# The attention's normalised rows: split as rows and turned by transposing transfers, instead of turned by TensorE and split from PSUM

## What is computed

```python
x = x + wkv_block(layernorm(x))     # k, r = h@Wk.T, h@Wr.T; scan over time per channel; sigmoid(r)*y @ Wo.T
x = x + ffn_block(layernorm(x))

def ffn_block(x):
    h = rmsnorm(x, gamma1)
    q = h @ Wq + bq                          # 16 heads of 32
    k, v = split((h @ Wdown + bdown) @ Wup + bup)   # latent of 64, then 16 heads
    att = softmax(q k^T / sqrt(32))          # between the 16 heads of one token
    x = x + att v @ Wo + bo
    h2 = rmsnorm(x, gamma2)
    return x + sum_e gate_e * (h2 @ We[e])   # 8 experts, all of them, dense
```

## Time and profile before

| | us |
|---|---|
| median of three runs | 2759.6 |
| the profiled execution, its time | 2758.6 |
| its span, first to last instruction | 2756.5 |
| TensorE busy with matmuls | 2586.4 (94%), 18896 matmuls |
| VectorE busy | 2133.6 (77%) |
| ScalarE busy | 1531.3 (56%) |
| GpSimd busy | 948.9 (34%) |
| mean granted TensorE clock | 0.975 of full speed |

### The profile page before, as it was taken

One profiled execution on the slowest core, in us unless ns is written; L12 is line 12 of the kernel. 1 busy time (PEld: TensorE's weight loads), 2 busy tenths in 40 slices (PEclk: granted clock), 3 DMA queues, 4 the chain that ended last, 5 costly groups with the idle time before them and its releaser, 6 DMA issues.

```text
span 2756.5 us, 48625 instructions
## 1 busy us (share of the span) xinstructions
PE 2586.4 (94%) x18896; PEld 1580.4 (57%) x18896; DVE 2133.6 (77%) x3647; ACT 1531.3 (56%) x2799; POOL 948.9 (34%) x970
## 2 busy tenths in 40 slices
PE   2458999999999999999999999999999999999999
PEld 2345566666556666655666665566666556655554
DVE  6677887788888778788877878887787888767743
ACT  5875555555555555555555555556555555654540
POOL 0453433333333333243333324333332433332420
PEclk7768999999999999999999999999999999999999
DMA  7202222211222221122222112222112222201220
GB/s 229 39 12 39 47 47 47 32 27 37 47 47 47 47 30 28 38 47 47 47 47 25 33 38 47 47 47 47 23 33 40 47 47 47 46 12 37 39 32 16
DMA packets 845322, 119.29 MB, mean 43 GB/s; under 512 B 813587, under 2 KB 813715, under 8 KB 845075
## 3 DMA queue, kind: packets, MB, share of 16 engines
q1 hardware_dynamic: 845092, 116.18, 22.9%
HBM read 48.49 MB, written 16.78 MB: 24 GB/s over the span
## 4 chain that ended last, share of the span: by engine, by line
PE 88%; DVE 4%; ACT 4%; POOL 2%; SPq 1%; issue 1%; DMA 0%; ACTq 0%; DVEq 0%; POOLq 0%
PE bank L1333 78%; PE bank L1355 3%; PE bank L1500 2%; PE bank L1471 2%; PE bank L1511 2%; DVE h2t L1104 1%; PE bank L1487 1%; POOL w_e L693 1%; ACT h2t L939 1%; PE bank L1512 1%; ACT ot L789 1%; DVE mcol L1234 0%; ACT t L888 0%; POOL pr L734 0%; DVE acc L1311 0%
## 5 line engine op out<-in xcount | busy, mean ns | idle before, releaser
L1333 PE MATMUL bank<-w_e,h2t 128*128 128x512 f16 x6144 | 1383.4, 380 | 2.8 <-DVE acc L1311 2.0
L1333 PEld LDWEIGHTS bank<-w_e,h2t 128*128 128x128 f16 x6144 | 592.1, 98 | 665.9 <-issue 4.4
L1311 DVE SCALAR_TENSOR_TENSOR acc<-bank,gates,acc 128x512 f32<-128x512 f32 x512 | 371.9, 736 | 120.4 <-PE bank L1333 117.4
L906 ACT ACTIVATE pr<-bank,plog,col 128x512 f32<-128x512 f32 x256 | 198.7, 776 | 407.9 <-PE bank L1500 405.5
L734 POOL TENSOR_TENSOR pr<-pr 128x512 f16<-128x512 f32 x256 | 295.7, 1160 | 182.3 <-ACT pr L908 180.9
L721 POOL TENSOR_TENSOR qo<-t,qo 128x256 f16<-128x256 f32 x128 | 106.5, 832 | 493.4 <-ACT qo L891 490.3
L1142 DVE TENSOR_TENSOR_SCAN wkv<-e,wkv 128x256 f32<-128x256 f32 x256 | 210.8, 864 | 74.6 <-ACT e L834 73.4
L1166 DVE RECIPROCAL zz<-zz 128x256 f32<-128x256 f32 x128 | 218.9, 1732 | 29.4 <-POOL zz L703 29.3
L1333 PE MATMUL bank<-w_o,xo 128*128 128x512 f16 x768 | 176.2, 387 | 46.9 <-DVE xo L1104 46.9
L908 ACT ACTIVATE pr<-bank,plog,col 128x512 f16<-128x512 f32 x256 | 197.8, 773 | 0.0
L1333 PE MATMUL bank<-xo,w_k 128*128 128x256 f16 x1536 | 172.9, 273 | 2.4 <-DVE xo L1104 2.4
(11 more groups left out here) (196 smaller groups left out, 3957.6 us busy)
## 6 DMA issues: line engine op xcount, KB each, us to landing
qs<-qo SPq DMA_DIRECT2D x384, 64.0 KB, 2.4
ks<-k SPq DMA_DIRECT2D x384, 64.0 KB, 2.4
xk<-in_attn_x SPq DMA_DIRECT2D x32, 512.0 KB, 4.0
x<-in_attn_x SPq DMA_DIRECT2D x32, 512.0 KB, 3.7
result<-acc SPq DMA_DIRECT2D x32, 512.0 KB, 2.8
w_e<-in_ffn_We SPq DMA_DIRECT2D x7, 1024.0 KB, 12.9
qs<-in_attn_Wk SPq DMA_DIRECT2D x1, 1024.0 KB, 7.9
ks<-in_attn_Wr SPq DMA_DIRECT2D x1, 1024.0 KB, 10.0
```

The source lines that it names most:

```text
L906: nc.scalar.activation(pr[:, k % 2, :], att_bank[ATT_BANK["S", k]][:, :], ACT.Exp, bias=plog[:, 0:1], scale=colof["soft"])\
L1311: V.scalar_tensor_tensor(out=acc[:, s, :], in0=moe_bank[u % 2][:, :], scalar=gates[:, s, e:e + 1], in1=acc[:, s, :], op0=ALU.mult, op1=ALU ...
L1333: ins = nc.tensor.matmul(dst, left(a), right(b), start=(n == 0), stop=(n == last))
```

## The change

ScalarE's `att_turn` no longer reads PSUM. It copies the rows `h_rows`, scaled, as fp16 into `hr16[:, 0, s]`; VectorE writes the rest into `hr16[:, 1, s]`. `hr16` is not a new buffer, it is `k16` under another shape; so ScalarE first waits until the stacking transfers of the tile before have read `k16`. SP then issues four transfers with `transpose=True` in a tile, each of 128 rows by 512 fp16 (128 KB), one for each `s` and half, into `ht16`. TensorE's `att_turn` is gone from its lists, `att_latent` waits for the four transfers, and the two uses T0 and T1 leave the ring of banks. SP's lists have a new step `att_turn` ahead of `att_up`. The orders of ScalarE, VectorE and GpSimd are as before.

```diff
-ATT_USES = ([("T", 0), ("T", 1), ("D", 0), ("Q", 0), ...
+ATT_USES = ([("D", 0), ("Q", 0), ...
 PE_ORDER
-    ... ("mix_k", 0, 1), ("att_turn", 0, 2), ("mix_v", 0, 1), ("att_latent", 0, 2), ...
+    ... ("mix_k", 0, 1), ("mix_v", 0, 1), ("att_latent", 0, 2), ...
 SP_ORDER = [
-    ("mix_k", 0, 2), ("att_m", 0, 3), ("att_up", 0, 2), ("pre_load", 0, 0), ("moe_store", 0, 4),
+    ("mix_k", 0, 2), ("att_m", 0, 3), ("att_turn", 0, 2), ("att_up", 0, 2), ("pre_load", 0, 0), ("moe_store", 0, 4),
+        hr16 = k16[:, :, :, :].rearrange("p l b t -> p l (b t)").rearrange("p l (s c) -> p l s c", s=SUB)
+        turn1_in = Steps(sem("turn1_in"), 16, h=4)
 # SP
+            def att_turn(t, _):
+                if t.back(1):
+                    sp.wait_ge(*att_dve.done(t.back(1), "vt"))
+                for s in range(SUB):
+                    for l, (steps, step) in enumerate(((att_act, "h_hi"), (att_dve, "h_lo"))):
+                        sp.wait_ge(*steps.done(t, step, s))
+                        sp.dma_start(ht16[:, l, :, s * P:(s + 1) * P], hr16[:, l, s, :], transpose=True).then_inc(turn1_in.sem, 16)
 # ScalarE
             def att_turn(t, _):
-                for b in range(2):
-                    act.wait_ge(*att_pe.done(t, f"T{b}"))
-                    nc.scalar.activation(ht16[:, 0, 2 * b:2 * b + 2, :], att_bank[ATT_BANK["T", b]][:, :], ACT.Copy, scale=XS)\
-                        .then_inc(att_act.sem, 1)
+                if t.back(1):
+                    act.wait_ge(*stack_in.done(t.back(1), "qk"))
+                for s in range(SUB):
+                    act.wait_ge(*att_act.done(t, "h", s))
+                    nc.scalar.activation(hr16[:, 0, s, :], h_rows[:, s, :], ACT.Copy, scale=XS).then_inc(att_act.sem, 1)
 # VectorE
             def att_turn(t, _):
-                for b in range(2):
-                    dve.wait_ge(*att_act.done(t, "h_hi", b))
-                    lo(ht16[:, 1, 2 * b:2 * b + 2, :], att_bank[ATT_BANK["T", b]][:, :], XS, ht16[:, 0, 2 * b:2 * b + 2, :])\
-                        .then_inc(att_dve.sem, 1)
+                for s in range(SUB):
+                    dve.wait_ge(*att_act.done(t, "h_hi", s))
+                    lo(hr16[:, 1, s, :], h_rows[:, s, :], XS, hr16[:, 0, s, :]).then_inc(att_dve.sem, 1)
 # TensorE
-            def att_turn(t, _):
-                pe.wait_ge(*att_act.done(t, "h"))
-                turn(h_rows, [att_bank[ATT_BANK["T", b]] for b in range(2)], att_pe, att_pe.sem, lambda b: att_free(t, "T", b))
             def att_latent(t, _):
-                pe.wait_ge(*att_dve.done(t, "h_lo"))
+                pe.wait_ge(*turn1_in.done(t, "h"))
```

More of the change, by code:

```diff
@@ L114, in blocks @@
     return range(CB) if name in ("d", "g") else range(2 * k, 2 * k + 2)
-ATT_USES = ([("T", 0), ("T", 1), ("D", 0), ("Q", 0), ("Q", 1), ("K", 0), ("K", 1), ("V", 0), ("V", 1),
+ATT_USES = ([("D", 0), ("Q", 0), ("Q", 1), ("K", 0), ("K", 1), ("V", 0), ("V", 1),
              ] + [("M", k) for k in range(8)] + [("S", 0)]
@@ L142 @@
     ("set_o1", 1, -1), ("mix_k", 0, 0), ("mix_v", 0, 0), ("mix_project", 0, 0), ("mix_turn", 0, 1), ("mix_k", 0, 1),
-    ("mix_v", 0, 1), ("att_turn", 0, 0), ("att_latent", 0, 0), ("att_q", 0, 0), ("att_up", 0, 0), ("att_max", 0, 0),
+    ("mix_v", 0, 1), ("att_latent", 0, 0), ("att_q", 0, 0), ("att_up", 0, 0), ("att_max", 0, 0),
     ("att_max", 1, 0), ("att_max", 2, 0), ("att_max", 3, 0), ("att_m", 0, 0), ("att_scores", 0, 0),
@@ L147 @@
     ("att_scores", 6, 0), ("att_probs", 5, 0), ("att_scores", 7, 0), ("mix_project", 0, 1), ("mix_turn", 0, 2),
-    ("att_probs", 6, 0), ("att_probs", 7, 0), ("mix_k", 0, 2), ("att_turn", 0, 1), ("mix_v", 0, 2),
+    ("att_probs", 6, 0), ("att_probs", 7, 0), ("mix_k", 0, 2), ("mix_v", 0, 2),
     ("att_latent", 0, 1), ("att_q", 0, 1), ("fin_project", 0, 0), ("att_up", 0, 1), ("fin_turn2", 0, 0),
@@ L158 @@
     ("att_probs", 4, 3), ("att_scores", 6, 3), ("att_probs", 5, 3), ("att_scores", 7, 3), ("mix_project", 0, 2),
-    ("att_probs", 6, 3), ("att_probs", 7, 3), ("mix_turn", 0, 1), ("moe", 9, 4), ("mix_k", 0, 1), ("att_turn", 0, 2),
-    ("mix_v", 0, 1), ("att_latent", 0, 2), ("att_q", 0, 2), ("moe", 10, 4), ("att_up", 0, 2), ("moe", 11, 4),
+    ("att_probs", 6, 3), ("att_probs", 7, 3), ("mix_turn", 0, 1), ("moe", 9, 4), ("mix_k", 0, 1), ("mix_v", 0, 1), ("att_latent", 0, 2), ("att_q", 0, 2), ("moe", 10, 4), ("att_up", 0, 2), ("moe", 11, 4),
     ("moe", 12, 4), ("fin_project", 0, 3), ("moe", 13, 4), ("moe", 14, 4), ("moe", 15, 4), ("fin_turn2", 0, 3),
@@ L171 @@
     ("moe", 9, 5), ("mix_turn", 0, 2), ("att_probs", 6, 4), ("att_probs", 7, 4), ("moe", 10, 5), ("mix_k", 0, 2),
-    ("mix_v", 0, 2), ("att_turn", 0, 3), ("fin_project", 0, 4), ("att_latent", 0, 3), ("att_q", 0, 3),
+    ("mix_v", 0, 2), ("fin_project", 0, 4), ("att_latent", 0, 3), ("att_q", 0, 3),
     ("att_up", 0, 3), ("moe", 11, 5), ("moe", 12, 5), ("moe", 13, 5), ("fin_turn2", 0, 4), ("moe", 14, 5),
@@ L179 @@
     ("att_probs", 5, 3), ("att_scores", 7, 3), ("moe", 8, 4), ("mix_turn", 0, 1), ("moe", 9, 4), ("att_probs", 6, 3),
-    ("att_probs", 7, 3), ("mix_k", 0, 1), ("mix_v", 0, 1), ("att_turn", 0, 2), ("moe", 10, 4), ("moe", 11, 4),
+    ("att_probs", 7, 3), ("mix_k", 0, 1), ("mix_v", 0, 1), ("moe", 10, 4), ("moe", 11, 4),
     ("att_latent", 0, 2), ("att_q", 0, 2), ("att_up", 0, 2), ("fin_project", 0, 3), ("moe", 12, 4), ("moe", 13, 4),
@@ L187 @@
     ("att_scores", 6, 2), ("att_probs", 5, 2), ("att_scores", 7, 2), ("mix_project", 0, 1), ("att_probs", 6, 2),
-    ("att_probs", 7, 2), ("moe", 7, 3), ("moe", 8, 3), ("moe", 9, 3), ("att_turn", 0, 1), ("moe", 10, 3),
+    ("att_probs", 7, 2), ("moe", 7, 3), ("moe", 8, 3), ("moe", 9, 3), ("moe", 10, 3),
     ("att_latent", 0, 1), ("att_q", 0, 1), ("att_up", 0, 1), ("fin_project", 0, 2), ("moe", 11, 3), ("moe", 12, 3),
@@ L379 @@
     ("pre_load", 0, 1), ("set_experts", 6, -1), ("set_experts", 7, -1), ("set_masks", 0, -1), ("mix_k", 0, 1),
-    ("att_up", 0, 0), ("att_m", 0, 0), ("pre_load", 0, 2), ("att_up", 0, 1), ("pre_load", 0, 3),
+    ("att_turn", 0, 0), ("att_up", 0, 0), ("att_m", 0, 0), ("pre_load", 0, 2), ("att_turn", 0, 1), ("att_up", 0, 1), ("pre_load", 0, 3),
 ]
 SP_ORDER = [
-    ("mix_k", 0, 2), ("att_m", 0, 3), ("att_up", 0, 2), ("pre_load", 0, 0), ("moe_store", 0, 4),
+    ("mix_k", 0, 2), ("att_m", 0, 3), ("att_turn", 0, 2), ("att_up", 0, 2), ("pre_load", 0, 0), ("moe_store", 0, 4),
 ]
 SP_TAIL = [
-    ("mix_k", 0, 3), ("att_m", 0, 4), ("att_up", 0, 3), ("pre_load", 0, 1), ("moe_store", 0, 5), ("mix_k", 0, 2),
-    ("att_m", 0, 3), ("att_up", 0, 2), ("moe_store", 0, 4), ("mix_k", 0, 1), ("att_m", 0, 2), ("att_up", 0, 1),
+    ("mix_k", 0, 3), ("att_m", 0, 4), ("att_turn", 0, 3), ("att_up", 0, 3), ("pre_load", 0, 1), ("moe_store", 0, 5), ("mix_k", 0, 2),
+    ("att_m", 0, 3), ("att_turn", 0, 2), ("att_up", 0, 2), ("moe_store", 0, 4), ("mix_k", 0, 1), ("att_m", 0, 2), ("att_turn", 0, 1), ("att_up", 0, 1),
     ("moe_store", 0, 3), ("att_m", 0, 1), ("moe_store", 0, 2), ("moe_store", 0, 1),
@@ L556, in att_reader @@
         def att_reader(use, k):
-            return {"T": (att_dve, "h_lo", k), "D": (att_act, "c", 0), "Q": (att_act, "q", 4 * k + 2),
+            return {"D": (att_act, "c", 0), "Q": (att_act, "q", 4 * k + 2),
                     "K": (att_act, "k", 4 * k + 2), "V": (att_act, "v", 2 * k + 1),
@@ L672, in _ @@
                      {"set_ident": set_ident, "set_load": set_load, "set_experts": set_experts, "set_masks": set_masks,
-                      "pre_load": pre_load, "mix_k": mix_k, "att_up": att_up, "att_m": att_m, "moe_store": moe_store})
+                      "pre_load": pre_load, "mix_k": mix_k, "att_turn": att_turn, "att_up": att_up, "att_m": att_m, "moe_store": moe_store})
             sp.wait_ge(*stored.done(Tile(NT - 1, 1, 0), "out"))
@@ L1549, in _ @@
                      {f"set_{name}": lambda _, k, name=name: set_turn(name, k) for name in TURNED} | {"mix_turn": mix_turn, "mix_k": mix_k, "mix_v": mix_v, "mix_project": mix_project,
-                          "att_turn": att_turn, "att_latent": att_latent, "att_q": att_q, "att_up": att_up, "att_max": att_max, "att_m": att_m, "att_scores": att_scores, "att_probs": att_probs,
+                          "att_latent": att_latent, "att_q": att_q, "att_up": att_up, "att_max": att_max, "att_m": att_m, "att_scores": att_scores, "att_probs": att_probs,
                           "fin_project": fin_project, "fin_turn2": fin_turn2,
```

## The result

The changed kernel takes 2904.9 us, the median of four runs (2900.1 to 2906.6), against 2759.6 us before: a ratio of 1.0525 with an interval of 1.0507 to 1.0543. It is slower, on the side and inside the range that were forecast; the forecast of 2860 us gave about two thirds of the loss: +100 against +145 us.

A forecast was written before the change was run, and what follows sets the result against it. TensorE was taken as the bound: stall less transposes over 28 tiles 68 us, tail 4.5, clock 34, together +106 us on the median of 2759.6, rounded down to 2860 us; range 2742 to 3040 us.

The forecast's parts named there:

- The removed transposes are worth 0.87 us a tile: TensorE's chain: the eight transposes of a tile cost 0.87 us; alone, their removal would give 27 us over 31 tiles.
- The stall, S = 3.3 us: Before att_latent: TensorE waits 3.3 us a tile for the last of the four transposing transfers.
- i: On SP: the spacing of two transposing transfers, taken as 1.1 us from the pace of small packets.
- L: The landing time of one transposing transfer, taken as 2.9 us.
- The clock, 1.2 us a tile: TensorE after the stall: half of a mean price of 2.5 us for a clock fall, 34 us over 28 tiles.
- Tiles 1 to 28 alike: Same sequence in each of these tiles: 28 x (3.3 - 0.87) = 68 us lost, plus the clock term.
- Tile 0 is covered: Head: tile 0 gains and loses nothing, since ScalarE comes to the latent's copy only at 116.89.
- The tail, 4.5 us: Last three tiles: somewhat more cover, stall 2.4 us and 1.5 us lost each, 4.5 us together.
- A, ordinary price: Before att_latent: transfers move like plain 64 KB ones, stall 1.6 us, +20 us, 2780 us; chance 0.22.
- B: Before att_latent: last transfer lands before TensorE arrives, or nearly; faster, 2733 us with full cover; chance 0.12.
- C: Before att_latent: transfers in 32 B pieces, stall 7.8 us and a clock fall each period, 3047 us; chance 0.16.
- D: Before att_latent: transfers turned block after block, none overlapped, stall 26 us, 3530 us; chance 0.05.

The follow-up runs named there:

- the best kernel: Changed kernel with halves made earlier, two transfers of 256 KB in place of four, and the same moves in head and tail lists: 2745.2 us, ratio 0.9950.
- the kernel with idle matmuls: Changed kernel with 24 idle matmuls in TensorE's list between mix_v and the wait for the four transfers: 2863.4 us, ratio 1.0376.
- the one with earlier halves: Changed kernel with ScalarE's and VectorE's att_turn earlier in the repeated lists and SP issuing the two hi transfers first: 2773.9 us, ratio 1.0053.
- the kernel with `moe 10`: Changed kernel with expert unit moe 10 moved ahead of att_latent in TensorE's repeated list, 2.6 us of cover: 2822.5 us, ratio 1.0228.

## Why the prediction was right, point by point

The side and the mechanism came out as forecast: a stall before `att_latent` for the last transfer, and slower matmuls after it. The size came out inside the range, with parts that were off in both directions.

- **TensorE is the bound, and each us of its waiting is lost.** Right. Without a wait the transfers cost nothing measurable (2759.1 us), with it the change costs 145 us.
- **The removed transposes are worth 0.87 us a tile.** Right: the best kernel's period is 80.58 - 79.88 = 0.70 us shorter in the mean, with a remnant of waits, and 0.83 us shorter where there is none (79.75 us, from `mcol` at 1040.90 to `mcol` at 1120.65). This also shows that the shorter ring of banks and ScalarE's new wait cost nothing to speak of, as the prediction had said from the lists.
- **The moved copies and subtractions cost nothing and cannot start earlier.** The first is right: 1.14 and 1.29 us, 0.08 us more for the four together and off TensorE. "Cannot" was right for these lists alone: the lists could be changed, and that is what undid the loss.
- **The stall, S = 3.3 us.** (The terms give 3.37.) Measured 3.57 in a period without a late transfer and 3.73 in the mean, with i = 1.28 in place of 1.1 and L = 2.54 in place of 2.9. The sum came out near by luck: an issue too short and a landing too long offset each other. I had let the packets' pace set i. The page shows 69632 packets (914724 - 845092 on the queue) and 16.8 MB more for 128 transfers, some 240 B a packet and not 64, and 717 - 631 = 86 us more of the 16 engines' time (24.7% of 2902 and 22.9% of 2756), 0.67 us a transfer. The engines had time to spare; it is the issue on SP that spaces the transfers, and it did not grow from 128 to 256 KB. I had rows for ordinary issues and did not ask whether a transposing one might take longer: it takes 1.26 us where they take 0.67.
- **The clock, 1.2 us a tile.** This term was too small: half a chance of 2.5 us was right neither in the chance nor in the price. I took half a chance, because 3.3 us lay under the 3.40 and 3.65 us of the earlier trace rows; the clock fell in 26 of 27 periods. The price is 1.7 us, by the kernel with idle matmuls; the two errors partly offset each other. The windows of two whole periods have a mean clock of 0.98 where one before had 1.00. The sign that I had named, a digit under 9 in the body, did not come: 2% of a period doesn't move a digit of the page. And the reasoning from the gap's length does not hold either way: gaps of 2.57 us were followed by a fall and one of 2.98 us was not.
- **Tiles 1 to 28 alike.** A period lost 4.70 us, where the terms gave 3.6; 27 x 1.07 us is 29 us. The whole gap between forecast and result is 45 us, of which 6 are the rounding of 2759.6 + 106 down to 2860; of the other 39 these 29 are the largest part. Of the 4.70, the mean wait less the transposes is 3.73 - 0.87 = 2.9 and the clock 1.6 (26 of 27 periods); 0.2 us is open.
- **Tile 0 is covered.** Wrong, the step that failed outright, though it is worth 3.3 us only. I looked at the latent's copy on ScalarE, which had room, and not at what follows TensorE's `att_q`. These rows, of before and after, show it:

```profile
140.63 3.79 PE L1487 MATMUL bank<-ks,qs 104*128 104x128 f16 x32 [18.71 <-DMA ks<-k]
```

```profile
114.16 2.74 PE L1342 MATMUL bank<-ht,w_d 128*128 128x256 f16 x12 [10.22 <-DMA ht<-k]
...
143.95 3.80 PE L1492 MATMUL bank<-ks,qs 104*128 104x128 f16 x32 [18.71 <-DMA ks<-k]
```

  The product came 5.5 us later and `att_max`, after the same wait of 18.71 us for the stacks, 3.3 us later. By the first turning of h2 (222.60 before, 229.92 after) the head had lost 7.3 us; the 4.0 us behind `att_max` hold tile 1, which the sum had at 3.6.
- **The tail, 4.5 us.** It lost what is left of 146, some 12 us. The waits there are 2.61, 2.01 and 4.02 us, less three times 0.87 is 6. The sum had no clock term for the tail; these windows, from the start of each of the three products on, show the fall after every one:

```profile
2597.30:2601.30 4.00, 4.00 (x25) 3.05 (x26) 0.22 (x1) 0.98 (x2) 0.00 (x0) 0.64 0.00 0
2687.70:2692.70 5.00, 4.96 (x31) 3.82 (x32) 4.90 (x9) 0.98 (x2) 1.65 (x1) 0.66 0.01 3
2766.70:2771.70 5.00, 5.00 (x31) 3.78 (x32) 1.35 (x3) 2.02 (x4) 0.00 (x0) 0.66 0.00 0
```

  What the clock held back in them, 0.36 x 4 + 0.34 x 5 + 0.34 x 5, is 4.8 us; with the 6 it makes 11 of the 12 us.
- **The rivals.** A, ordinary price: wrong by the issue and by having no fall of the clock. Its range began at 2757 us, but by its own terms L = 2.1 gives 2771 us. Its landing was right, 2.5 against 2.4 us. By that the rule of the Trainium skill (Advanced Engine Details and Errata, § X-Bar Transpose (TRN2)) agrees with the landing in this trace; it says nothing on the issue, which decided. B could have been had: the version with earlier halves and two transfers is B, at 0.5% and not 1%. C and D are out. The 1309 ns for a 128x128 block (VectorE: DVE Perf Modes, § The three transpose paths, in the Trainium skill) does not add up block after block here, where 16 blocks landed some 6.4 us after the first issue, three issues of 1.28 and one landing of 2.54.

## What to carry to other kernels

When work leaves the bounding engine for a transfer, don't compare the two durations but lay the whole new chain (last operand ready, issues one after the other, one landing) against the moment at which that engine arrives. Here, from the last half on (1048.75), TensorE arrived after 1.5 us (1050.21) and the last transfer had landed after 5.0 us (1053.73). If the room is missing, look first at what stands before the operand in the lists of engines that are not the bound: making it earlier, with two transfers in place of four, turned +145 into -14 us, while of the work moved in between on the bounding engine a part was taken back at the next tight waits. And price a gap on TensorE with the slower matmuls after it, not by its length alone.

## What the runs showed of the hardware that was not expected

- A transposing transfer holds SP's queue for about 1.26 us, whether it carries 128 or 256 KB (medians 1264 and 1281 ns), about twice an ordinary one of 64 KB (671 ns). It lands 2.5 us (128 KB) or 3.3 us (256 KB) after its issue, in the median; single issues took up to 2.2 us and single landings up to 4.5 us in the changed kernel. Of the two sizes tried, fewer and larger was better: two for a tile instead of four took 62 us off the changed kernel and 17 us off the one with earlier halves.
- The same gap on TensorE can be followed by a fall to 1.2 GHz or not. After gaps of 2.5 to 3.6 us in the kernel with two transfers the clock fell in 11 of 27 periods, after gaps of 3.6 to 4.5 us in the changed kernel in 26 of 27, after gaps of 0.95 to 2.04 us in the kernel with idle matmuls once, after the longest. Even the wait of 1.67 us for the stacks in one period of the kernel with `moe 10` was followed by a fall:

```profile
1305.42 1.07 PE L1492 MATMUL bank<-ks,qs 104*128 104x128 f16 x16 [1.67 <-DMA ks<-k]
...
1306.80:1310.20 3.40, 3.40 (x19) 1.30 (x17) 2.98 (x9) 1.26 (x4) 2.39 (x2) 0.50 0.01 5
```

  Longer gaps are followed more often, but the length alone does not decide; what else does is open. The fall can come after work has started again (0.96 in the microsecond in which it starts at 1053.78, then 0.50) and before: in the tail of the old kernel the clock is 0.88 from 2490 to 2491, and work starts at 2491.47.
- Matmuls whose operand a transposing transfer wrote run as fast as those whose operand ScalarE and VectorE wrote: 273 ns with `w_d` in the repeated part of the last kernel, 273 ns in the median of the kernel before.
